# Third layer of a four-layer network: the stream of the binary network starts at slot 0 of the retention's timetable instead of three of its own steps later

## The reference, cut to what matters

```python
def _L2_attn_ref(x, W_ret, b_ret, ...):          # "retention", 4 x 1024 tokens of 256
    sig = sigmoid(x @ W_ret + b_ret)
    ret = scan over time: xi = 0.5 * s_t + 0.5 * xi
    h = layernorm(x + ret, ln1)
    ffn = gelu(h @ W1 + b1) @ W2 + b2            # 256 -> 1024 -> 256
    return layernorm(h + ffn, ln2)

def _L2_ffn_ref(x, k0, k1, k2, s0, s1, s2):      # "binary", same tokens
    h = s0 * (concat([x, -x]) @ sign(k0))        # 512 -> 1024
    h = relu(h) * 2
    h = s1 * (h @ sign(k1))                      # 1024 -> 1024
    h = relu(h) * 2
    return s2 * (h @ sign(k2))                   # 1024 -> 256

xn = layernorm(x)
x = x + _L2_attn_ref(xn, ...) + _L2_ffn_ref(xn, ...)
```

## Time and profile before

| What | Value |
|---|---|
| median of 3 runs | 3845.64 us (3840.07 to 3855.26) |
| profiled execution, span from first to last instruction | 3867.5 us |
| PE busy in it | 3519.2 us, 91% |
| DVE, ACT, POOL busy | 2473.4, 1730.0, 1164.8 us |
| mean granted TensorE clock | 0.937 of full |

### The profile page before, as it was taken

The page is one execution under the profiler, slowest core; times in us unless marked ns, Lnnn a source line. Parts: engine busy times, 40 slices in busy tenths (PEclk is TensorE's granted clock), DMA queues, the critical chain, the costliest instruction groups (busy, mean ns, idle before and its releaser), DMA issues.

```text
span 3867.5 us, 47778 instructions
## 1 busy us (share of the span) xinstructions
PE 3519.2 (91%) x16468; PEld 2089.1 (54%) x16468; DVE 2473.4 (64%) x6381; ACT 1730.0 (45%) x3237; POOL 1164.8 (30%) x1190
## 2 busy tenths in 40 slices
PE   8899999968898988989878999998899999999998
PEld 7677777734555545545546667676543333433332
DVE  4444443455788988889865443443568788678774
ACT  2234443322234423343344544443346666666667
POOL 0322222151355555555542322223211111011111
PEclk7799999988899999999989999999889899999999
DMA  3244445321466666666750000000101011111100
GB/s 109 73 165 168 177 180 180 128 66 71 136 204 193 216 211 194 197 204 197 212 187 3 0 1 1 1 1 9 38 20 31 20 23 34 31 34 27 32 18 23
DMA packets 107154, 368.87 MB, mean 95 GB/s; under 512 B 27248, under 2 KB 41088, under 8 KB 96928
## 3 DMA queue, kind: packets, MB, share of 16 engines
q0 software_dynamic: 57664, 302.82, 24.3%
q1 hardware_dynamic: 48160, 60.90, 5.6%
q10 hardware_dynamic: 1088, 2.10, 0.2%
HBM read 322.59 MB, written 17.69 MB: 88 GB/s over the span
## 4 chain that ended last, share of the span: by engine, by line
PE 66%; DVE 21%; ACT 6%; issue 4%; another core or an unknown queue 2%; POOL 1%; DMA 0%; POOLq 0%; DVEq 0%; SPq 0%; ACTq 0%
PE ps L184 51%; PE ps L2636 6%; DVE pm L2784 4%; PE ps L1507 2%; DVE mi L1642 2%; DVE gathB L1719 2%; DVE ps L2787 2%; DVE hacc L1682 2%; ACT P L2917 1%; PE ps L2126 1%; DVE mx L1638 1%; PE ps L556 1%; PE ps L581 1%; PE ps L546 1%
## 5 line engine op out<-in xcount | busy, mean ns | idle before, releaser
L2917 ACT ACTIVATE P<-ps 128x512 f32<-128x512 f32 (+3 forms) x1280 | 587.3, 548 | 214.1 <-PE ps L184 212.0
L2784 DVE TENSOR_REDUCE pm<-ps 128x1 f32<-128x512 f32 x768 | 484.6, 684 | 113.3 <-PE ps L184 113.0
L1860 POOL DMA_INDIRECT gathB<-in_tab,idx x256 | 282.9, 1105 | 357.6 <-PE ps L1507 287.4
L184 PE MATMUL ps<-QS,KS 49*128 49x512 f32 (+3 forms) x1280 | 333.8, 422 | 16.2 <-DVE pm L2784 12.6
L1860 POOL DMA_INDIRECT gathA<-in_tab,idx x256 | 268.7, 1049 | 203.2 <-DVE mx L1638 125.5
L184 PE MATMUL ps<-KS,QS 48*128 48x512 f32 (+3 forms) x1280 | 309.8, 430 | 16.0 <-DVE pm L2787 5.9
L2974 POOL TENSOR_SCALAR_AFFINE_SELECT P<-P 128x256 f32<-128x256 f32 x256 | 103.8, 409 | 709.9 <-ACT P L2917 709.0
L2636 PE MATMUL ps<-P,Va 128*32 128x512 f32 (+3 forms) x2560 | 309.7, 557 | 5.8 <-POOL P L2974 2.9
L184 PEld LDWEIGHTS ps<-QS,KS 49*128 49x128 f32 x1280 | 158.2, 190 | 225.0 <-DVE pm L2784 81.8
L184 PEld LDWEIGHTS ps<-KS,QS 48*128 48x128 f32 x1280 | 145.5, 191 | 212.8 <-DVE pm L2784 66.2
L2787 DVE CUSTOM_DVE_ANT_0 ps<-ps,past 128x128 f32<-128x128 f32 (+3 forms) x512 | 240.1, 515 | 26.6 <-PE ps L184 24.6
(11 more groups left out here) (390 smaller groups left out, 7002.8 us busy)
## 6 DMA issues: line engine op xcount, KB each, us to landing
ys_sorted<-moe SPq DMA_DIRECT2D x71, 128.0 KB
KS<-hi SPq DMA_DIRECT2D x256, 32.0 KB, 1.9
QS<-hi SPq DMA_DIRECT2D x256, 32.0 KB, 1.9
gathA<-in_tab,idx POOLq DMA_INDIRECT x256
gathB<-in_tab,idx POOLq DMA_INDIRECT x256
KS<-lo SPq DMA_DIRECT2D x128, 32.0 KB, 1.9
QS<-lo SPq DMA_DIRECT2D x128, 32.0 KB, 2.0
out<-xT SPq DMA_DIRECT2D x8, 512.0 KB, 3.2
```

The costliest lines, as they stand in the source:

```text
L184: m = pe.matmul(out, w, x, start=start and i == 0, stop=stop and i == len(pairs) - 1, skip_group_check=True)
L1860: pool.indirect_dma_start(out=(GA, GB)[half][:, h, :], out_offset=None, in_=d[f"tab{half}"], in_offset=bass.IndirectOffsetOnAxis(ap=idx[t ...
L2784: v = dve.tensor_reduce(m, p, AX.X, ALU.max)
L2917: act.activation(P_[:, hh, off:BW], psx.tile("s2", j, n, kt, pr, hh)[:, off:BW], ACT.Exp).then_inc(*psx.emptied(MN.act, "s2", j, n, kt, pr ...
```

## The change

One number: `LATE` goes from 3 to 0. No instruction of arithmetic is added or removed; the merged lists of PE, DVE and ACT are in another order, and POOL's list is the same.

```diff
-            SLOTS, LATE, BINARY = 27, 3, 1.93
+            SLOTS, LATE, BINARY = 27, 0, 1.93
```

## The result

The changed kernel takes 3900.48 us (median of 4 runs, 3891.63 to 3905.26) against 3848.27 us of the kernel before on the same chip: a ratio of 1.0121, with an interval of 1.0091 to 1.0151. That is 47 us by the ratio and 52 by the medians. The forecast was 3884 us, range 3858 to 3908, slower.

What follows compares the result with a forecast made beforehand. TensorE (PE) was taken to bound the layer, so only its idle time and clock count. Six boundaries 27.6, the seventh 3.5, clock 8.1, start -1: +38.2 us on 3845.6 gives 3884 us, range 3858 to 3908.

Steps and rivals of the forecast that it cites:

- The boundary: From one binary-network block to the next: PE idle 9.25 us with the wait before y0, against 4.7 before; +4.6 us each.
- yb_7: At the boundary, only yb_6 stands beside its chain through ACT, DVE and POOL, so PE waits 1.7 us.
- varl: Norm's matmul behind yb_7: its chain of subtraction, squares and `rest` leaves PE idle 0.5 us.
- f1_2 and f1_3: Matmul columns of f1 that wait for ACT's relus to empty two banks: 1.2 and 0.1 us idle.
- f1_6 and f1_7: Columns of f1 whose banks stay full while ACT's squares hold back the relus: 2.15 and 0.2 us idle.
- f2_0: Reads all eight f1 columns, so it waits for ACT's last relus and POOL's subtraction: 2.25 us idle.
- rf: Wait of y0 behind ACT's first gelu, the relu of f2_1 and a table load: 1.15 us instead of 0.69.
- The clock: Falls at six of seven boundaries, each costing 1.7 us of slow f2_0 matmuls, against three before costing 0.7: +8.1 us.
- Rival 1: Clock stays at the lower level through the whole boundary: 57.5 us slower, 3903 us; chance 0.18.
- The seventh boundary: From block 6 to block 7, without varl: 8.0 us idle against 4.5 before, +3.5 us.
- The start: f1 matmuls fill the 7.69 us gap ahead of `mu1`, but K1 parts and queued relus delay f2_0: -1 us.
- The end: Layer's dense binary tail is done beside the retention's work, saving nothing; yb_7 ends it with the same wait: 0.

Runs made afterwards that it cites:

- split_later: Changed kernel with DVE's cast and POOL's subtraction of xa for the next block moved ahead of f2_4's; layer 731.9 us instead of 742.
- w2_early: Changed kernel with the low part of W2 made right behind the low part of W1 in block 0; layer 738.7 us, 3.5 shorter.
- sq_behind: As w2_early, with the first norm's squares behind all eight f1 relu pairs on ACT, its rest and variance a step later; layer 729.7 us.
- one_relu: Changed kernel with ACT's first relu of each f1 column left out; three blocks take 85.3 us, the three with `mu1` ahead of f1_2 88.7 to 89.6.

## Why the prediction was right, and where it was off

The mechanism, the sign and the range held. How near the sum came is in part luck, because some of its terms were too small and others too large. Point by point, by its own steps:

- **The boundary.** Forecast 9.25 us idle, measured 7.92 at the one shown and 7.7 to 9.1 at the six. Forecast and measured at the one shown: yb_7 1.7 and 1.71; `varl` 0.5 and 0.46; f1_2 and f1_3 1.3 and 0.73; f1_6 and f1_7 2.35 and 1.76; f2_0 2.25 and 1.05 (1.96 at five of the seven); `rf` 1.15 and 2.21; `rsql` 0 and 0. Over the six blocks between the sigmoid's matmuls PE's idle time went from 494.28 - 467.41 = 26.9 to 533.24 - 481.54 = 51.7 us: +24.8, forecast 27.6.
- **`rf`** was the term of the boundary sized too small. The step "same chain of durations" took `rf` at 0.69 from a place where POOL was idle. Here the first `rf` took 1.43 beside POOL, and split_later, which moves POOL's work away, has it at 0.69 again and y0's wait at 1.42. The slow cast doesn't count, since DVE waits for the gelu behind it. The waits for f1 and f2_0 were sized too large, by 0.3 to 1.2 us each, so that the sum came out near.
- **The clock** was also too small: matmuls were busy 14.1 us longer in the six blocks, where I had 8.1 for seven boundaries. I had counted six falls, each on the matmuls of f2_0. There are eleven in this trace: one behind the 2.2 us of `rf` at each of the first six boundaries, four more ahead of it at the first three, and one at yb_7 of the last. A block with the one fall behind `rf` has PE busy 79.5 us, against 77.5 in a block of the kernel before without a fall: 2.0 us for one, where I had 1.7, and nothing of it is given back. A fall ahead of f2_0, as at the boundary shown, is given back in part: f2_0 then waits 1.05 and not 1.96. Where the falls lie is not fixed: at the second boundary of the second trace of this kernel there is a single one, at f2_0, as I had drawn it. Rival 1, a low clock through the whole boundary, did not come: the windows from 2220 to 2236 are at 1.00.
- **The seventh boundary:** forecast +3.5, measured +3.3. The tail of the layer, from the last sigmoid's matmuls, went from 117.3 to 107.5 us, with three f2 columns and three yb (14.0 us) fewer in it: +4.2, of which 0.9 is the end.
- **The start** was on the wrong side: -1 forecast, +3.7 measured (101.5 us to the second sigmoid's matmuls against 83.8, with those 14.0 more in it). The idle time before `mu1` is gone, as forecast, but 8.5 us of it stand ahead of f1_6 instead. The layer starts 1.0 us earlier in this trace; measured from there the squares are 1.2 us behind the forecast, with four parts of K1 at 6.84 us where rows 6 had 4.66. The step that failed is the next one, the relus behind them, which the forecast lets start at once: they wait 3.04 us for the low part of W2, which no step of it names. f2_0 is 3.9 us late by then. w2_early takes 2.3 us of the start back; the rest was not tested.
- **The end:** 0 forecast, +0.9: the last yb waits 2.35 and not 1.71, the first matmul of the next layer 8.38 and not 8.10. The first is a matter of DVE's order: its addition of the retention's branch to x (1.23 us, L2227) now stands right ahead of the cast of f2_7, which starts only when it is done, where before DVE waited for ACT's relu. At the seventh boundary it is the same, with a wait of 2.36. The second I didn't follow.
- The sum: 39.0 for six blocks + 3.3 + 3.7 + 0.9 = 46.9 us. Against 38.2 forecast the miss is the clock in the blocks (`rf`, too small, and the other waits, too large, nearly cancel) and the start.
- Two of the signs named beforehand did not come as said: PE's waits for POOL ahead of f2_0 are 1.05 to 1.96 us and not 2 to 2.5, and those for ACT's relus 1.3 to 2.5 us for a boundary and not 3 to 4.
- One reading of the order was too coarse: I took the shown boundary for all. In the last four of the seven, `mu1` stands ahead of f1_2. It did little harm here, 9.1 us of idle time for a block against 8.8 at the third boundary. In sq_behind and one_relu such a block is some 3 us longer than the first ones: 0.9 and 1.4 us of that is idle time, the rest a lower clock.

The rule of the Trainium skill ("TensorE: Matmul & The Clock Gate", section "A second HAM failure mode: psum-queue depth-cycling") says that short idle times between groups of matmuls, as PE cycles through PSUM banks, make the clock swing. The trace agrees: every one of the seven boundaries has a fall, where 3 had one before, and I had counted on six. It gives no price that these runs could be held against.

## What to carry to other kernels

When two streams are woven into one in-order list, their offset decides what stands between a producer and its consumer at the one place where both have a chain of small steps. Walk that place engine by engine, with the durations from a stretch in which the same neighbours are busy, and don't expect a line between two values: none, one and two steps late gave 742, 751 and 715 us. An engine that is the bound gains nothing by having its dense tail done earlier: here 14.0 us of matmuls left the tail and came back at the start. And split each gain into idle time and busy time of the bound engine before you credit it to a wait: in split_later and sq_behind about half of it was the clock.

## What the runs showed of the hardware

VectorE's steps between buffers in SBUF took longer while GpSimd was at work. A cast of 0.43 us took 2.39, beside a subtraction of 2.50 us on GpSimd; two subtractions of 0.69 took 1.43 and 1.74, and `rf` was back at 0.69 where GpSimd's work was moved away. It is not one factor: in each case the VectorE step ends 0.3 to 0.5 us behind the GpSimd step that was running when it started. The cast that had started 0.17 us ahead of GpSimd's subtraction kept its 0.43. What a step costs thus depends on what GpSimd is in the middle of. The signs K1, written from 8-bit inputs, show the same at the changed kernel's start. DVE's timeline there, where POOL's four subtractions ran from 2039.2 to 2045.9:

```profile
2039.62 6.84 DVE L2017 TENSOR_SCALAR K<-raw 128x1024 fp32r<-128x1024 uint8 x4
...
2047.51 1.28 DVE L2017 TENSOR_SCALAR K<-raw 128x1024 fp32r<-128x1024 uint8 x2
```

That is 1.7 us for one beside GpSimd and 0.64 alone, and each of the four again ends 0.5 us behind a subtraction of GpSimd. GpSimd was slowed less: its four took 6.74 us together, 1.7 each, against 1.27 alone.

At each boundary of the changed kernel, whose six blocks have 7.7 to 9.1 us of idle time, the granted clock fell at least once, and in the kernel before, with 4.7 us, at 3 of 7. The idle time alone doesn't say it: two blocks of sq_behind have 7.5 us of it and no fall. One fall cost 1.2 to 2.0 us of busy time, and two traces of the same kernel differ in where the falls lie.
